# Sorted output experts of a two-layer attention kernel: the last pair's step moves into the next batch, tables are made later, one store per chunk

## The chip, the core and the metric

The kernel runs as one launch on one core of a Trainium2 chip. The metric is the device time of a launch in microseconds, lower is better. The core has five engines that run their own instruction streams and meet through semaphores: TensorE (PE: matmuls, and transposes done as matmuls), VectorE (DVE), ScalarE (ACT), GpSimd (POOL) and SyncE (SP, which here only issues transfers). PSUM is the accumulator memory, eight banks of 2 KB in each of 128 partitions; SBUF is the core's own memory, DRAM holds inputs, outputs and the scratch tables.

## The reference

Four batches of 512 tokens with 256 features go through two layers. The change touches the second step of the first layer:

```python
x = x + xattn(layernorm(x), ctx)               # one head, 1601 keys, softmax in fp32
# L0 ffn: 8 heads of 64, 8 experts per head
q, k = heads(x @ w_q), heads(x @ w_k)
gates = sigmoid(heads(x @ w_gate))             # (b, h, n, e)
gm = one_hot(argmax(gates, -1), 8) * gates     # one expert per head and token
values = einsum('bhne,ehdk,bnd->bhnk', gm, value_experts, x)
out = einsum('bhij,bhjk->bhik', softmax(causal(q @ k.T / 8)), values)
out = einsum('bhne,ehkd,bhnk->bhnd', gm, output_experts, out)
x = x + out.sum(axis=1)                        # sum over the heads
# then layer 1: 16-head attention over ctx with a mask, and a mixture of 32 experts
```

Every token picks one output expert in each head. Its row of 64 numbers is multiplied with that expert's 64x256 matrix alone, and the eight results are added to x.

## The kernel before

Everything here is in `attentions_ab`. For each batch b, TensorE runs `attention_a(b)` (the first attention, L766 scores, L779 transposes of probabilities, L798 context matmuls, L820), then `head_b(b)` (transposes of the normalised x at L867, gates at L874, queries and keys), then `attention_b(b)`: the 8 heads in four pairs. The value experts are 32 "units" of four 128x512 matmuls (L1056): eight before pair 0, and eight in each of pairs 0 to 2. VectorE takes each unit with the gates (L1511, L1515). Pair p's attention (transposes L929, value matmuls L1025) ends with `turn_rows`. The fourth pair (`last_pair`) has no units; the scores of the next batch's first tile stand between its parts.

In batches 0 to 2 (`SORTED` = 3) the output experts are done by sorting. Q = 4b + p numbers the pairs, EARLIER = 12. The steps of a pair:

- VectorE weighs the rows and writes them (`weigh`, `write_rows`, L1627). GpSimd scatters them to `sorted_in` in DRAM with eight indirect transfers (L677), to the places that the table `to_sorted` gives, so that blocks of 128 rows have one expert.
- SyncE loads for each of the 11 blocks and 2 heads of the pair the matrix of its expert, 22 transfers with an address read from the table `of_block` (`load_experts`, L605), and behind them the sorted rows (`load_sorted`, L615). The loads wait until the whole table is there, and until the blocks of pair Q-2 are multiplied.
- TensorE transposes the rows (`turn_sorted`, three groups, L970), ScalarE copies them out (`read_sorted`, L1365). TensorE multiplies two blocks at a time (`out_sorted`, six chunks c = 0 to 5, L992, bank 6 and 7), ScalarE copies each chunk out (`read_blocks`, L1379) and issues two stores of it to `sorted_out` (L1384). The buffers alternate, so a copy waits for the stores of the chunk two before.
- GpSimd gathers the results in the tokens' order (eight indirect transfers, L692, table `from_sorted`) once every store of the pair has landed (`all_kept`), and VectorE adds them to x (`add_back`, L1637).

TensorE's part of pair Q-1 stands in pair Q: pairs 0, 1 and 2 of a batch are multiplied in pairs 1, 2 and 3. Pair 3's part stands in `sorted_between(b + 1)`, between the next batch's `attention_a` and `head_b`, alone in its place. In `last_pair` ScalarE has all six chunks of pair 2 ahead of the next batch's first softmax (L1325; the maximum it needs is L1484). Batch 3 doesn't sort; it follows another scheme (`pair`, `ending_pair`).

The tables are made once a batch, by `place` on VectorE in five pieces, one behind each of the units 3 to 7 before pair 0 (L1573 to L1609; the last one, L1600 to L1609, gives `of_block`). They come from counts that TensorE makes by matmuls in bank 3. `placed` counts their 23 instructions. In batch 2 GpSimd normalises batch 0's x for the second layer (L146) behind `all_kept(7)`, TensorE transposes it at L820; the statistics for it (`statistics`) are taken on VectorE at the end of batch 1's pair 1. SyncE writes the finished x away in `keep_x`.

The context matmuls at L798 share bank 6 with the chunks: they wait for the same copies. `head_b` waits with its gates (bank 6) for the copies of all blocks so far.

## Time and profile before

| | us |
|---|---|
| median of 3 runs | 2146.98 |
| lowest, highest | 2142.21, 2147.06 |
| the profiled execution | 2155.61 |
| its span | 2153.8 |

The mean granted clock of TensorE is 0.95 of full speed. The rows below are of the profiled execution, in microseconds from the start of its span. The heads of batches 0 to 2 begin at 184, 419 and 683 (in the last two with the expert block of pair 3 ahead); behind 970 follow batch 3's experts and the second layer, which the diff doesn't touch.

### The profile page before, as it was taken

What the parts mean: (1) busy time and instruction counts of PE and PEld (TensorE: products, weight loads), DVE (VectorE), ACT (ScalarE), POOL (GpSimd) and SP (SyncE); (2) the same over time, 40 slices, a digit from 0 to 9 for tenths busy, and PEclk for the clock granted to TensorE, in tenths of its full rate; (3) what the DMA queues carried; (4) which work ended last, traced back from release to release, by engine and by line L of the source; (5) the groups of instructions that cost most, each with busy time, mean ns of one, the idle gap of its engine ahead of it and who ended that gap; (6) DMA issues with size and microseconds to landing.
All of it is one profiled execution on the core that took longest, in us unless ns stands there. A gap on an engine that the chain in (4) does not pass through costs nothing. (4 is left out here: it accounts for less than half of the span.)

```text
span 2153.8 us, 29336 instructions
## 1 busy us (share of the span) xinstructions
PE 1934.9 (90%) x10024; PEld 1024.5 (48%) x10024; DVE 1250.2 (58%) x2553; ACT 980.3 (46%) x1899; POOL 729.6 (34%) x660
## 2 busy tenths in 40 slices
PE   8989897988888888889998999999999999986993
PEld 5666344744456444565563333343343333335772
DVE  5434752266522665239877767778777877742342
ACT  3412242212323123222105879778877887861220
POOL 4330143104433054211106133224632541326575
PEclk9999998989989999899998999999999999997997
DMA  8741156214633046351125374337542643105997
GB/s 284 208 161 56 56 180 196 87 42 118 195 116 120 27 129 189 97 168 51 55 31 134 80 243 114 64 68 176 113 107 39 174 79 49 50 26 181 267 193 164
DMA packets 184077, 262.88 MB, mean 122 GB/s; under 512 B 48135, under 2 KB 140117, under 8 KB 182648
## 3 DMA queue, kind: packets, MB, share of 16 engines
q1 hardware_dynamic: 121208, 179.21, 30.9%
q0 software_dynamic: 26624, 47.18, 8.8%
q10 hardware_dynamic: 36096, 34.61, 4.9%
q8 instruction: 80, 1.31, 0.3%
q14 instruction: 69, 0.57, 0.1%
HBM read 165.92 MB, written 104.44 MB: 126 GB/s over the span
## 5 line engine op out<-in xcount | busy, mean ns | idle before, releaser
L2623 ACT ACTIVATE d_prob<-ps 128x512 f32<-128x512 f32 (+1 forms) x832 | 473.5, 597 | 155.2 <-PE ps L2473 154.4
L2650 DVE CUSTOM_DVE_ANT_0 ps<-ps,maskN 128x801 f32<-128x801 f32 x480 | 467.6, 1015 | 125.6 <-PE ps L2443 125.4
L1056 PE MATMUL ps<-vx_or_keys,b_xT 128*128 128x512 f32 x512 | 253.5, 623 | 19.1 <-DVE val_or_prob L1511 18.9
L2485 PE MATMUL ps<-d_prob,vaug 128*32 128x512 f32 (+1 forms) x1664 | 225.9, 609 | 0.3 <-ACT d_prob L2623 0.3
L692 POOL DMA_INDIRECT val_or_prob<-sorted_out,oxB x96 | 98.7, 1028 | 359.6 <-DVE xx L1637 160.7
L2472 PE MATMUL ps<-maskT,identb 128*128 128x512 bf16 (+1 forms) x498 | 192.0, 385 | 4.4 <-POOL maskT L2347 2.5
L2619 ACT CAST ps<-maskT 128x512 f32<-128x512 bf16 (+1 forms) x310 | 185.5, 598 | 0.0
L265 POOL DMA_INDIRECT table<-xr,slot x128 | 128.4, 1004 | 168.4 <-PE ps L2473 133.2
L1350 ACT ACTIVATE prob_or_gate<-ps,b_mx 128x512 f32<-128x512 f32 (+3 forms) x128 | 66.1, 525 | 187.8 <-DVE b_mx L1502 185.8
L1511 DVE TENSOR_TENSOR val_or_prob<-ps,b_gm 128x512 f32<-128x512 f32 x128 | 88.2, 689 | 103.4 <-PE ps L1056 101.6
L1056 PEld LDWEIGHTS ps<-vx_or_keys,b_xT 128*128 128x128 f32 x512 | 92.1, 195 | 114.1 <-issue 79.1
L1515 DVE TENSOR_REDUCE val_or_prob<-val_or_prob 128x64 f32<-128x512 f32 x128 | 132.4, 1034 | 4.4
L677 POOL DMA_INDIRECT sorted_in<-oxB x96 | 95.7, 997 | 110.0 <-DVE oxB L1627 81.4
L992 PE MATMUL ps<-oxB,og_or_pT 64*128 64x256 f32 x528 | 86.8, 452 | 41.8 <-ACT og_or_pT L1379 27.8
L2347 POOL TENSOR_SCALAR maskT<-c_rawT 128x512 bf16<-128x512 int32 (+1 forms) x52 | 100.2, 1926 | 50.9 <-PE ps L2473 43.2
L2473 PE MATMUL ps<-raw,kS 99*128 99x512 bf16 (+1 forms) x312 | 115.6, 387 | 1.4 <-ACT ps L2619 1.4
L2472 PEld LDWEIGHTS ps<-maskT,identb 128*128 128x128 bf16 (+1 forms) x498 | 49.7, 100 | 121.4 <-issue 34.2
L766 PE MATMUL ps<-maskN,kS 128*128 128x512 f32 (+1 forms) x256 | 101.3, 545 | 1.7 <-PEq L103 1.7
L2473 PE MATMUL ps<-qS,vx_or_keys 99*128 99x512 bf16 (+1 forms) x260 | 99.3, 386 | 1.9 <-ACT ps L2619 1.9
L2473 PE MATMUL ps<-vx_or_keys 99*128 99x512 bf16 (+1 forms) x260 | 98.3, 382 | 1.9 <-ACT ps L2619 1.9
L798 PE MATMUL ps<-og_or_pT,raw 128*128 128x128 f32 (+1 forms) x832 | 97.6, 275 | 0.0
L798 PEld LDWEIGHTS ps<-og_or_pT,raw 128*128 128x128 f32 (+1 forms) x832 | 95.4, 192 | 1.5 <-issue 1.5
(356 smaller groups left out, 3153.7 us busy)
## 6 DMA issues: line engine op xcount, KB each, us to landing
sorted_out<-og_or_pT ACTq DMA_DIRECT2D x90, 256.0 KB
oxB<-in_B_ox SPq DMA_DIRECT2D x264, 64.0 KB
c_rawT<-in_maskT SPq DMA_DIRECT2D x24, 512.0 KB
vx_or_keys<-k_parts SPq DMA_DIRECT2D x60, 200.1 KB, 7.1
k_parts<-x_k SPq DMA_DIRECT2D x16, 600.4 KB
table<-xr POOLq DMA_DIRECT2D x16, 578.0 KB
e_buf<-table SPq DMA_DIRECT2D x32, 289.0 KB, 4.0
oxB<-sorted_in SPq DMA_DIRECT2D x12, 704.0 KB, 5.4
```

The costliest lines, as they stand in the source:

```text
L265: g.indirect_dma_start(out=k.table[:, :], out_offset=bass.IndirectOffsetOnAxis(ap=k.slot[:, j:j + 1], axis=0), in_=k.xr[:, t, :], in_offse ...
L766: mm = pe.matmul(ps[:, i, 0:KC[i]], k.qkA[:, c, t * P:(t + 1) * P], k.ctxTA[:, c, i * BANK:i * BANK + KC[i]], start=c == 0, stop=c == NC - 1)
L798: mm = pe.matmul(ps[:, 6, m * P:(m + 1) * P], k.ctxNA[0:KW[i], i, m * P:(m + 1) * P], pT[0:KW[i], i, :], start=i == 0 and m == 0, stop=i = ...
L1056: mm = pe.matmul(ps[:, bank, :], xTB[:, c, t * P:(t + 1) * P], vxB[:, c, h, :], start=c == 0, stop=c == NC - 1)
L1515: v.tensor_reduce(val[:, t, h // 2 % 2, h % 2, :], tmp[:, u % 2, :].rearrange("p (e d) -> p d e", e=EB), AX_X, ALU.add).then_inc(val_sum, 1)
L2347: g.tensor_scalar(maskT[0:KW[i], i, :], rawT[0:KW[i], u % 2, i % 2, :], 0.0, MASKED, ALU.is_equal, ALU.mult).then_inc(biasT, 1)
L2472: pe.matmul(ps[0:w, BANKS[u], :], k.identb[0:w, 0:w], maskT[0:w, i, :], start=True, stop=False)
L2473: pe.matmul(ps[0:w, BANKS[u], :], kS[G % NS][0:KROWS + 3, h, i * P:i * P + w], qS[G % NS][0:KROWS + 3, h, :], start=False, stop=True, skip ...
L2485: mm = pe.matmul(ps[VW * h:VW * (h + 1), ACC, :], vaug[0:w, G % 2, i, h, :], prob[0:w, T % 2, h, :], start=i == 0, stop=i == NKT - 1)
L2619: nc.scalar.copy(ps[0:w, BANKS[later], :], maskT[0:w, i, :]).then_inc(mask_a, 1)
L2623: nc.scalar.activation(prob[0:w, T % 2, h, :], ps[0:w, BANKS[GH * T + h], :], ACT.Exp, scale=SCALE_C).then_inc(exped, 1)
L2650: v.tensor_tensor_reduce(banks, banks, maskN[:, t, MO[half]:MO[half] + w], 1.0, -3.0e38, ALU.add, ALU.max, mp[:, t, h, half:half + 1]).the ...
```

## The change

- Pair 3's sorted work is done in pair 0 of the next batch, in the places where pairs 1 and 2 have that of the pair before. `sorted_between` is left for batch 3 alone.
- Chunks 4 and 5 of pair 2 move from `last_pair` into the next `attention_a`; ScalarE copies them behind the softmax of tiles 0 and 1. The rest of `last_pair` is put in another order.
- Each chunk is stored with one transfer: the two heads' rows lie side by side in `sorted_out`. The table `from_sorted` goes, `to_sorted` serves both ways.
- GpSimd gathers tiles 0 and 1 before a pair's scatter, 2 and 3 behind it (in a batch's last pair all before). VectorE adds the later two in the next pair.
- Table pieces: the second moves from behind unit 4 to behind unit 5, the last three move into pair 0 (behind unit 9, unit 10 and the written rows). The counts are in bank 5.
- The statistics and `keep_x` move from pair 1 to pair 2. Head, GpSimd and VectorE waits are set to what is done by then.

```diff
-PLACING = 23
+PLACING = 21
...
-        to_sorted, from_sorted, of_block = ([x.bitcast(I32) for x in part[i:i + 2]] for i in (3, 5, 7))
+        to_sorted, of_block = ([x.bitcast(I32) for x in part[i:i + 2]] for i in (3, 5))
...
@@ sync
-                        if p == 1 and b >= 1:
+                        if p == 2 and b >= 1:
                             keep_x(b - 1)
@@ gpsimd, in gather: for t in tiles, in_offset from to_sorted
-                    if b >= 1 and p < 2:
-                        gather(PAIRS * b - 2 + p)
-                    if b < SORTED:
-                        if p >= 2:
-                            gather(PAIRS * b - 2 + p)
+                    Q = PAIRS * b + p
+                    if b == SORTED:
+                        if p < 2:
+                            gather(Q - 2, range(NT))
+                    else:
+                        ahead = 2 if p + 1 < PAIRS else NT
+                        if Q >= 2:
+                            gather(Q - 2, range(ahead))
                         scatter(b, p)
+                        if Q >= 2:
+                            gather(Q - 2, range(ahead, NT))
@@ tensor, attention_a
+                    if b and i == 1:
+                        out_sorted(PAIRS * b - 2, 4)
                     if i < NT and (b == 0 or i >= 1):
                         for j in range(NKC):
                             scores(b, i, j)
+                    if b and i == 1:
+                        out_sorted(PAIRS * b - 2, 5)
...
@@ tensor, head_b
-                pe.wait_ge(blocks_a, CHUNKS * PAIRS * b)
+                if b:
+                    pe.wait_ge(blocks_a, CHUNKS * (PAIRS * b - 1 if b < SORTED else PAIRS * b))
@@ tensor, turn_b; values gets the wait on placed
-                if g == 0 and p == 0 and b < SORTED:
-                    pe.wait_ge(placed, PLACING * b + 13)
...
@@ tensor, counts: bank 3 becomes bank 5
...
@@ tensor, sorted_pair (all nine places)
-                if p:
+                if Q:
                     turn_sorted(Q - 1, 0)
...
@@ tensor, last_pair
                 turn_sorted(Q - 1, 1)
+                turn_sorted(Q - 1, 2)
                 scores(b + 1, 0, 1)
                 turn_rows(b, p)
-                turn_sorted(Q - 1, 2)
+                out_sorted(Q - 1, 0)
                 scores(b + 1, 0, 2)
-                out_sorted(Q - 1, 0)
                 out_sorted(Q - 1, 1)
                 scores(b + 1, 0, 3)
-                for c in range(2, CHUNKS):
-                    out_sorted(Q - 1, c)
+                out_sorted(Q - 1, 2)
+                out_sorted(Q - 1, 3)
...
@@ tensor and scalar, the loop over batches
-                if b:
+                if b == SORTED:
                     sorted_between(b)
@@ scalar, attention_a, behind the softmax of tile i
+                    if b and i < 2:
+                        read_blocks(PAIRS * b - 2, 4 + i)
@@ scalar, read_blocks
-                    act.wait_ge(kept[c % 2], 32 * (n // 2))
+                    act.wait_ge(kept[c % 2], 16 * (n // 2))
+                if c == 0 and not between:
+                    act.wait_ge(placed, PLACING * ((Q + 1) // PAIRS + 1))
...
-                for a in range(2):
-                    half = k.sorted_out[Q % 2][ROWS * a:ROWS * (a + 1), :].rearrange("(j p) n -> p j n", p=P)
-                    nc.scalar.dma_start(half[:, 2 * c:2 * c + w, :], o[:, a, 0:w, :]).then_inc(kept[c % 2], 16)
+                nc.scalar.dma_start(k.sorted_out[Q % 2].rearrange("(j p a) n -> p j (a n)", p=P, a=2)[:, 2 * c:2 * c + w, :],
+                                    o[:, 0:w].rearrange("p j a n -> p j (a n)")).then_inc(kept[c % 2], 16)
@@ vector, sorted_pair
+                if p and Q >= 3:
+                    add_back(Q - 3, 2)
+                    add_back(Q - 3, 3)
+                if p == 0:
+                    place(b, 2)
                 weigh(b, p)
                 maxima(b, p + 1, 0)
                 unit(b, u + 2)
-                add(0)
+                if p == 0:
+                    place(b, 3)
+                if Q >= 2:
+                    add_back(Q - 2, 0)
                 unit(b, u + 3)
                 write_rows(b, p)
-                add(1)
+                if Q >= 2:
+                    add_back(Q - 2, 1)
+                if p == 0:
+                    place(b, 4)
...
-                add(3)
-                if Q == PAIRS + 1:
+                if Q == PAIRS + 2:
                     v.wait_ge(added, 2 * NT * PAIRS)
                     statistics(v, nq, k.xx[0][:, :, :])
```

TensorE, from the end of batch 0's last pair into batch 1's `attention_a`. L766 are scores, L992 the chunks (a row with x4 is one chunk of two blocks, x2 the last one), L779 the transposes of probabilities, L798 the context matmuls. Before:

```order
L766 MATMUL ps<-maskN,kS 128x512 x2
L992 MATMUL ps<-oxB,og_or_pT 128x256 x8
L766 MATMUL ps<-maskN,kS 128x65 x2
L992 MATMUL ps<-oxB,og_or_pT 128x256 x14
L779 MATMUL ps<-ident,val_or_prob 128x128 x8
L766 MATMUL ps<-maskN,kS 128x512 x6
L766 MATMUL ps<-maskN,kS 128x65 x2
L779 MATMUL ps<-ident,val_or_prob 128x128 x4
L798 MATMUL ps<-og_or_pT,raw 128x128 x16
L779 MATMUL ps<-ident,val_or_prob 65x128
L798 MATMUL ps<-og_or_pT,raw 128x128 x10
```

With the change (L774, L1003, L787 and L806 are the same lines moved; L965 is `turn_rows`):

```order
L1003 MATMUL ps<-oxB,og_or_pT 128x256 x4
L774 MATMUL ps<-maskN,kS 128x512 x2
L1003 MATMUL ps<-oxB,og_or_pT 128x256 x4
L774 MATMUL ps<-maskN,kS 128x65 x2
L1003 MATMUL ps<-oxB,og_or_pT 128x256 x8
L787 MATMUL ps<-ident,val_or_prob 128x128 x8
L1003 MATMUL ps<-oxB,og_or_pT 128x256 x4
L774 MATMUL ps<-maskN,kS 128x512 x6
L774 MATMUL ps<-maskN,kS 128x65 x2
L1003 MATMUL ps<-oxB,og_or_pT 128x256 x2
L787 MATMUL ps<-ident,val_or_prob 128x128 x4
L806 MATMUL ps<-og_or_pT,raw 128x128 x16
```

All six chunks stood ahead of the first probability transposes; now four do, one chunk stands behind the first transposes, and the last one (x2) behind the scores of tile 1, directly ahead of further transposes and the context matmuls.

TensorE, from the end of batch 1's `attention_a` into `head_b(1)`. L416 is the last of the attention, L867 (L879) the head's transposes. Before:

```order
L416 MATMUL ps<-bkA,b_kT 128x1 x8
L970 MATMUL ps<-ident,oxB 128x128 x11
L992 MATMUL ps<-oxB,og_or_pT 128x256 x22
L867 MATMUL ps<-ident,og_or_pT 128x128 x8
L874 MATMUL ps<-wgB,b_xT 128x64 x8
L884 MATMUL ps<-b_xT,wqB 128x512 x2
L884 MATMUL ps<-b_xT,wkB 128x512 x2
```

With the change:

```order
L820 MATMUL ps<-kS,og_or_pT 128x256 x2
L411 MATMUL ps<-b_kT,kS 128x512 x4
L416 MATMUL ps<-bkA,b_kT 128x1 x8
L879 MATMUL ps<-ident,og_or_pT 128x128 x8
L887 MATMUL ps<-wgB,b_xT 128x64 x8
L897 MATMUL ps<-b_xT,wqB 128x512 x2
L897 MATMUL ps<-b_xT,wkB 128x512 x2
```

The 11 transposes and 22 block matmuls between L416 and the head are gone from here.

VectorE, the last table piece of batch 1 (L1600, L1603, L1607, L1609). L1511 and L1515 take a unit. Before, ahead of pair 0:

```order
L1597 TENSOR_SCALAR oxB<-og_or_pT 128x16 x4
L1511 TENSOR_TENSOR val_or_prob<-ps,b_gm 128x512
L1515 TENSOR_REDUCE val_or_prob<-val_or_prob 128x64
L1600 TENSOR_TENSOR og_or_pT<-og_or_pT 128x64
L1603 TENSOR_TENSOR og_or_pT<-og_or_pT,oxB 128x704
L1607 TENSOR_REDUCE og_or_pT<-og_or_pT 128x88
L1609 TENSOR_SCALAR oxB<-og_or_pT 128x88
L1511 TENSOR_TENSOR val_or_prob<-ps,b_gm 128x512
L1515 TENSOR_REDUCE val_or_prob<-val_or_prob 128x64
```

With the change (the piece is L1613 to L1622; L1609 is the piece with `to_sorted`, L1650 `add_back`, L1640 the written rows, L1525 and L1529 a unit):

```order
L1609 TENSOR_SCALAR oxB<-og_or_pT 128x16 x2
L1650 TENSOR_TENSOR xx<-xx,val_or_prob 128x256 x2
L1525 TENSOR_TENSOR val_or_prob<-ps,b_gm 128x512
L1529 TENSOR_REDUCE val_or_prob<-val_or_prob 128x64
L1640 TENSOR_TENSOR oxB<-ps,b_gr 128x512
L1650 TENSOR_TENSOR xx<-xx,val_or_prob 128x256 x2
L1613 TENSOR_TENSOR og_or_pT<-og_or_pT 128x64
L1616 TENSOR_TENSOR og_or_pT<-og_or_pT,oxB 128x704
L1620 TENSOR_REDUCE og_or_pT<-og_or_pT 128x88
L1622 TENSOR_SCALAR oxB<-og_or_pT 128x88
L1525 TENSOR_TENSOR val_or_prob<-ps,b_gm 128x512
```

The table that the expert loads wait for is now complete behind the written rows of pair 0, and no longer behind unit 7.

## Rows read from the trace of the kernel before

**Rows 1.** Page, part 1: busy us (share of the span) xinstructions, by engine.

```profile
PE 1934.9 (90%) x10024; PEld 1024.5 (48%) x10024; DVE 1250.2 (58%) x2553; ACT 980.3 (46%) x1899; POOL 729.6 (34%) x660
```

**Rows 2.** Waits, PE, 180-970: engine line <- waited for: us, times, longest.

```profile
PE ps L992 <- ACT og_or_pT L1379: 27.8, 26, 1.9
...
PE ps L992 <- ACT val_or_prob L1379: 11.0, 10, 3.3
```

**Rows 3.** Timeline, PE (start, us, line, operation, count [idle before <- releaser]).

```profile
184.83 1.07 PE L867 MATMUL ps<-ident,og_or_pT 128*128 128x128 f32 x8
...
202.32 1.88 PE L1056 MATMUL ps<-vx_or_keys,b_xT 128*128 128x512 f32 x4
...
419.12 1.07 PE L970 MATMUL ps<-ident,oxB 128*128 128x128 f32 x8
...
454.38 1.88 PE L1056 MATMUL ps<-vx_or_keys,b_xT 128*128 128x512 f32 x4
...
682.81 1.07 PE L970 MATMUL ps<-ident,oxB 128*128 128x128 f32 x8
...
720.21 1.88 PE L1056 MATMUL ps<-vx_or_keys,b_xT 128*128 128x512 f32 x4
```

**Rows 4.** Timeline, ACT: the first softmax of batches 1, 2 and 3.

```profile
355.92 1.60 ACT L1325 ACTIVATE val_or_prob<-ps,a_mx 128x1601 f32<-128x1601 f32 x1 [1.78 <-issue]
...
615.26 1.60 ACT L1325 ACTIVATE val_or_prob<-ps,a_mx 128x1601 f32<-128x1601 f32 x1 [1.02 <-issue]
...
877.62 1.60 ACT L1325 ACTIVATE val_or_prob<-ps,a_mx 128x1601 f32<-128x1601 f32 x1 [0.97 <-ACT og_or_pT L1379]
```

**Rows 5.** Timeline, batch 2: ACT's second softmax, PE's first context matmuls.

```profile
628.67 1.60 ACT L1325 ACTIVATE val_or_prob<-ps,a_mx 128x1601 f32<-128x1601 f32 x1 [9.08 <-DVE a_mx L1484]
...
626.61 3.74 PE L798 MATMUL ps<-og_or_pT,raw 128*128 128x128 f32 x32
```

**Rows 6.** Timeline, batch 2: POOL normalises xx, PE transposes it.

```profile
619.42 4.85 POOL L146 TENSOR_SCALAR og_or_pT<-xx,norm_nc_mv,norm_nc_rstd 128x256 f32<-128x256 f32 x4 [6.06 <-DMA sorted_out<-og_or_pT]
...
630.19 0.60 PE L820 MATMUL ps<-ident,og_or_pT 128*128 128x128 f32 x4
```

**Rows 7.** Timeline, ACT, batch 3's block: two stores, a copy.

```profile
939.15 0.89 ACTq L1384 DMA_DIRECT2D sorted_out<-val_or_prob  x2
...
942.40 1.01 ACT L1379 COPY val_or_prob<-ps 128x1024 f32<-128x1024 f32 x1 [1.01 <-DMA sorted_out<-val_or_prob]
```

**Rows 8.** Timeline, SP's issues: slices and rows of pairs 0, 2, batch 0.

```profile
229.05 27.57 SPq L605 DMA_DIRECT2D oxB<-in_B_ox  x22
256.84 0.41 SPq L615 DMA_DIRECT2D oxB<-sorted_in  x1
...
324.45 30.20 SPq L605 DMA_DIRECT2D oxB<-in_B_ox  x22
```

**Rows 9.** Timeline, PE: pair 0's first sorted transposes, batches 0 and 2.

```profile
261.87 0.66 PE L970 MATMUL ps<-ident,oxB 128*128 128x128 f32 x4 [0.53 <-DMA oxB<-sorted_in]
...
781.66 0.66 PE L970 MATMUL ps<-ident,oxB 128*128 128x128 f32 x4 [3.70 <-DMA oxB<-sorted_in]
```

**Rows 10.** Timeline, DVE, batch 0: last table piece, rows of pairs 0, 1.

```profile
225.31 0.21 DVE L1600 TENSOR_TENSOR og_or_pT<-og_or_pT 128x64 f32<-128x64 f32 x1
...
227.40 0.20 DVE L1609 TENSOR_SCALAR oxB<-og_or_pT 128x88 int32<-128x88 f32 x1
...
243.47 0.68 DVE L1627 TENSOR_TENSOR oxB<-ps,b_gr 128x512 f32<-128x512 f32 x1
...
271.91 0.68 DVE L1627 TENSOR_TENSOR oxB<-ps,b_gr 128x512 f32<-128x512 f32 x1
```

**Rows 11.** Windows: us, busy of PE, PEld, DVE, ACT, POOL; PEclk; DMA; GB/s.

```profile
781.70:787.00 5.30, 5.30 (x16) 2.05 (x17) 1.23 (x1) 2.04 (x5) 0.00 (x0) 0.68 0.29 80
261.90:265.50 3.60, 3.60 (x14) 1.45 (x14) 2.55 (x5) 0.92 (x2) 0.00 (x0) 1.00 0.17 51
```

**Rows 12.** Timeline, PE, batch 1: first transposes of pair 2.

```profile
549.69 0.66 PE L929 MATMUL ps<-ident,prob_or_gate 128*128 128x128 f32 x4 [2.02 <-DVE b_pT L1714]
```

125 lines of the change are left out of this document (61 added, 64 removed).

## The prediction

> **What bounds the kernel now.** I read the page's engine line first, then TensorE's waits in the stage that holds the experts, then the timelines of the five engines there. TensorE is busy 90% of the span, no other engine above 58% [rows 1], so a change pays where it takes work or a wait off TensorE's row. In the stretch from the first gates to the last batch's head (180 to 970 us) TensorE waits 27.8 + 11.0 us in 36 places for ScalarE's copies of expert blocks [rows 2], and it waits for a batch's first softmax and for sorted rows to land [rows 4, 9]. These are what the change touches. Everything after 970 us should shift as a whole: nothing there is edited.
>
> All sums below are against the profiled execution (2155.61 us, span 2153.8), which lies 8.6 above the median of the runs, 2146.98; the difference found is then put on the median.
>
> **1. The block between attention and head goes, for batches 1 and 2.** In batch 0, which has no such block, the head takes 17.49 us from its first transpose (184.83) to the first value unit (202.32). In batches 1 and 2 the same way, with the last pair's expert block ahead of it, takes 454.38 - 419.12 = 35.26 and 720.21 - 682.81 = 37.40 us [rows 3]. Both should fall to 17.49, the waits for ScalarE's last blocks and for the input copied behind them included. Gain 17.77 + 19.91 = **37.7 us**. Batch 3 keeps its block.
>
> **2. The end of the last pair.** Today the batch's first softmax waits in ScalarE's queue behind six blocks and twelve stores: it starts at 355.92, 615.26 and 877.62, in the first two cases with no idle wait for its input [rows 4]. After, only four blocks stand ahead, with one store each. By my count ScalarE would be through with block 3 and its store at 346.1 (the 1.01 us copies, a 0.44 us issue each, matmuls of 1.13 us), and VectorE gives the maximum at about 345.8, since the gathers start some 1.6 us earlier once the last store is one issue and no load of sorted rows competes with it. The softmax starts near 346.1, 606.3 and 868.9. Gain 9.8 + 9.0 + 8.7 = **27.5 us**.
>
> **3. Chunks 4 and 5 come back in the attention.** Chunk 4 costs TensorE 1.07 us. Chunk 5 stands behind the scores of tile 1, and it brings a new wait: the context matmuls (L798) write bank 6 and wait until every block of that pair is copied out. ScalarE copies chunk 5 only after the softmax of tile 1. In batch 2 that softmax ends at 630.27, and the context matmuls start at 626.61 [rows 5]; a one-block copy (0.59 us, half of 1.01 and some start cost) and the signals would free them at 631.0. So 1.1 + 4.4 = 5.5 us a batch, three times: **16.5 us** lost. Queued behind the waiting matmul is TensorE's whole attention.
>
> **4. Batch 2's normalisation of the kept input.** GpSimd normalises xx for the next layer only when all stores of that pair have landed. Today this ends at 624.27, before its transpose (L820, 630.19) [rows 6]. After, the store of chunk 5 goes out at about 632.5, lands 2.3 us later (as the quiet stores of batch 3 do: issue ends 940.04, the next copy it gates starts 942.40 [rows 7]), and 4.85 us of normalising follow [rows 6]: some 639.8. TensorE comes there at 635.7. **4.1 us** lost.
>
> **5. Tables made later: the large cost.** SyncE loads the 22 expert slices of a pair in one loop, each with an address read from the table, and only behind them in its queue the sorted rows. The loop starts about 1 us after the last table instruction and takes 27.6 to 30.2 us [rows 8]. In batch 0 the table is done at 227.60 (227.40 + 0.20), the slices are issued from 229.05 to 256.62, the rows at 256.84, and TensorE takes them at 261.87 after a 0.53 us wait [rows 8, 9]. So 34.3 us from table to rows, and this chain already ends last: in batch 2 TensorE waits 3.70 us there [rows 9]. The scatter, which batches 1 and 2 also wait for, comes clear of it after the change. Now the table's last piece (225.31 to 227.60, 2.29 us [rows 10]) moves from before pair 0 to behind that pair's rows.
> Where does it end? From the first value unit of the batch, the units reach pair 0's last transpose group in 28.2 us (31.4 today in batch 0, with three pieces of table between the units on VectorE; I take 1.5 us off for the last unit, 1.1 for VectorE being free for the transposes' copies, and leave half of the low clock). In batch 0 VectorE then goes through pair 0 as now (write of the rows ends at 244.15, 10.4 us behind that group [rows 10]) and needs 2.3 us more: 28.2 + 12.6 = 40.8. Plus 34.3: 75.1 us against 59.55 today (261.87 - 202.32), so 15.5 later. In batches 1 and 2 pair 0 has the sorted work too, like pair 1 of batch 0, where the write of rows starts at 271.91: 28.2 + 14.65 + 34.3 = 77.15 against 61.45 in batch 2 (781.66 - 720.21 [rows 3, 9]), and I take batch 1 alike: 15.7 later each. Total **46.9 us** lost. That is net of the sooner units, and it hides all TensorE work that the change adds to pair 0 (11 transposes and 22 blocks): the wait in pair 1 grows to some 12 us in batches 1 and 2 and 18 in batch 0. The later pairs have slack again: SyncE's loop for pair 1 starts right behind, and is through 5 us before its rows are wanted.
>
> **6. The clock.** After its 3.70 us of waiting the stretch from the sorted transposes to the value matmuls takes 5.3 us where batch 0, after 0.53, needs 3.6, at a granted clock of 0.68 against 1.00 [rows 9, 11]: a level between 1.2 and 2.4 GHz on average. Batch 0 now pays such a stretch, and waits of 12 to 18 us may cost up to 3 us, nearly twice that. I take 2.5 for batch 0, 0.9 more for each of batches 1 and 2, and 3.9 for the four new waits of points 3 and 4: **8.2 us** lost. On this the Trainium skill (TensorE: Matmul & The Clock Gate, Why this matters for your kernels) says that idle gaps between bursts of matmuls return TensorE to the half rate; the trace agrees on 5.3 against 3.6 us.
>
> **7. One store per chunk, gathers, statistics.** An issue takes 0.44 us on ScalarE (0.89 for two [rows 7]), and one of two goes. Most waits for block copies are for work ahead of the copy, not for the store, so I take 1.5 us in the pairs and 2.0 in batch 3's block. Moving the statistics of xx from pair 1's end to pair 2's removes a 2.02 us wait and the slow unit behind it [rows 12]: 2.4. Gathers split around the scatters cost nothing: GpSimd's waits are in front of its scatters, and the additions fit into VectorE's gaps. Gain **5.9 us**. The Trainium skill (DMA: Bandwidth & Descriptors, Anatomy of one DMA) puts most of a transfer's fixed 2.0 us into the write's receipt, none of which a merged store saves; by it only the issue is gained, as taken here.
>
> **Sum:** -37.7 - 27.5 + 16.5 + 4.1 + 46.9 + 8.2 - 5.9 = +4.6 us. Profiled 2160.2; on the median **2151.6 us**, 0.2% slower, which a measurement cannot tell from no change (0.3%, 6.4 us).
>
> **Rivals.**
> A, slower: the clock. If each of the seven long waits costs 3.3 us, twice the 1.7 of rows 11, and SyncE's loop runs at its 30.2 us beside stores and scatters rather than 27.6, that is 7 x 3.3 - 8.2 = 15 and 3 x 2.6 = 8 more: up to 2174; half of it gives 2163. It decides from 1.8 us beyond my sum, where 2153.4 is passed. For it: the second loop, beside scatters, does take 30.2 us [rows 8]. Against: the loop of pair 0 is the quickest one now.
> B, faster: stores bind. If half an issue and a quicker landing count at each of 36 block waits (38.8 us [rows 2]), 0.45 x 36 = 16 us go instead of 3.5: 2139. For it: a copy of a block waits 1.01 us for a store's landing [rows 7]. Against: in the pairs most of them wait for TensorE.
> C, the gains come whole and the table's delay is hidden (rows could be loaded without waiting for the slices): 2146.98 - 50 = 2097. Against it is SyncE's order, unchanged: slices, then rows. I give it 3%.
>
> **Chances.** My sum 60%, A 20%, B 17%, C 3%. The case of my sum spans 2145 to 2158 and passes 2153.4 a quarter of the time, so it gives 0.45 to no change and 0.15 to slower; B gives 0.01 to no change. Same 0.46, slower 0.15 + 0.20 = 0.35, faster 0.16 + 0.03 = 0.19. The range that holds 8 in 10 reaches into A and B: 2138 to 2166.
>
> **What would show it.** The profile after should have TensorE's first sorted transposes in pair 1 wait 15 to 19 us in batch 0 and 10 to 14 in batches 1 and 2, for the load of sorted rows; no expert block between the attention and the head of batches 1 and 2, and 17.5 us for that head; about 3.3 us of waiting ahead of L798's first context matmul of batches 1 to 3; some 4 us ahead of the transpose of the kept input. I am wrong if the wait in pair 1 stays under 8 us (then faster), or if new waits appear in pairs 2 and 3 (then slower).

## The result

The changed kernel is slower than the one before: 2171.86 us (median; 2168.06 to 2175.55) against 2147.02 (2142.21 to 2151.10), a ratio of 1.0116 with a 95% interval of 1.0086 to 1.0147. The forecast was 2151.6 with a range of 2138 to 2166: it expected a difference too small to measure, and the time lies above the range. The profiled execution took 2168.06 us, its span is 2166.2. That is 12.4 more than the span before; up to the first value unit of batch 3, where the edited part ends, it is 20.8 us behind (987.18 against 966.36). The part behind it was 8.4 us shorter in this execution than in that of before, which lay 8.6 above its own median; that part took 1177 to 1185 us in the traces of the first eight experiments, so it varies by that much from one execution to the next. So the 20.8 us are what has to be explained, and they are close to the 24.8 between the medians.

TensorE's waits in the edited stretch of the changed kernel (engine, line, waited for: us, times, longest); the lines answer to [rows 2]:

```profile
PE ps L981 <- DMA oxB<-sorted_in: 51.3, 5, 17.3
PE ps L1003 <- ACT og_or_pT L1394: 23.4, 24, 1.6
PE ps L787 <- ACT val_or_prob L1338: 13.0, 3, 5.9
...
PE ps L806 <- ACT og_or_pT L1394: 10.3, 3, 3.4
...
PE ps L1003 <- ACT val_or_prob L1394: 2.3, 4, 1.2
```

L1003 is L992 of before, L787 L779, L806 L798, L981 L970. The waits for block copies fell from 38.8 to 25.7 us. The wait for sorted rows was before, from 180 to 970 us:

```profile
PE ps L970 <- DMA oxB<-sorted_in: 8.9, 5, 3.7
```

It rose from 8.9 to 51.3 us, and 10.3 us are new ahead of the context matmuls.

TensorE's timeline: heads and first units of batches 1 and 2 (answering to [rows 3]), and pair 0's sorted rows in each batch with the value matmuls behind the first ([rows 9]).

```profile
277.31 1.12 PE L981 MATMUL ps<-ident,oxB 128*128 128x128 f32 x4 [17.32 <-DMA oxB<-sorted_in]
...
283.11 2.38 PE L1038 MATMUL ps<-b_pT,val_or_prob 128*64 128x512 f32 x16
...
438.06 1.07 PE L879 MATMUL ps<-ident,og_or_pT 128*128 128x128 f32 x8
...
455.56 1.88 PE L1069 MATMUL ps<-vx_or_keys,b_xT 128*128 128x512 f32 x4
...
535.13 1.11 PE L981 MATMUL ps<-ident,oxB 128*128 128x128 f32 x4 [14.13 <-DMA oxB<-sorted_in]
...
704.68 1.07 PE L879 MATMUL ps<-ident,og_or_pT 128*128 128x128 f32 x8
...
722.18 1.88 PE L1069 MATMUL ps<-vx_or_keys,b_xT 128*128 128x512 f32 x4
...
801.78 1.11 PE L981 MATMUL ps<-ident,oxB 128*128 128x128 f32 x4 [13.87 <-DMA oxB<-sorted_in]
```

Both heads take 17.50 us, where 35.26 and 37.40 were. The three waits for rows are 17.32, 14.13 and 13.87 us; forecast were 15 to 19 and twice 10 to 14.

The end of the table on VectorE, and SyncE's loop and load behind it ([rows 8, 10]):

```profile
243.41 0.20 DVE L1622 TENSOR_SCALAR oxB<-og_or_pT 128x88 int32<-128x88 f32 x1
...
498.62 0.20 DVE L1622 TENSOR_SCALAR oxB<-og_or_pT 128x88 int32<-128x88 f32 x1
```

```profile
245.06 27.13 SPq L608 DMA_DIRECT2D oxB<-in_B_ox  x22
272.25 0.57 SPq L618 DMA_DIRECT2D oxB<-sorted_in  x1
...
499.73 29.83 SPq L608 DMA_DIRECT2D oxB<-in_B_ox  x22
529.66 0.53 SPq L618 DMA_DIRECT2D oxB<-sorted_in  x1
```

From batch 0's first unit (202.74) to the end of the table are 40.87 us (forecast: 40.8). In batch 1 (455.56 to 498.82) they are 43.3, forecast 42.85. The loop took 27.13 us in batch 0, but 29.83 in batch 1, and 29.83 in batch 2.

The first softmax of batch 2, with what stands ahead of it on ScalarE and on VectorE ([rows 4]):

```profile
622.23 1.01 ACT L1394 COPY og_or_pT<-ps 128x1024 f32<-128x1024 f32 x1 [1.97 <-DMA sorted_out<-og_or_pT]
...
625.63 1.60 ACT L1338 ACTIVATE val_or_prob<-ps,a_mx 128x1601 f32<-128x1601 f32 x1 [2.39 <-DVE a_mx L1498]
```

```profile
622.53 0.88 DVE L1650 TENSOR_TENSOR kS<-kS,val_or_prob 128x256 f32<-128x256 f32 x2 [1.47 <-DMA val_or_prob<-sorted_out,oxB]
```

The second softmax of batch 1, ScalarE's copy of chunk 5 behind it, and TensorE's context matmuls ([rows 5]):

```profile
382.30 1.60 ACT L1338 ACTIVATE val_or_prob<-ps,a_mx 128x1601 f32<-128x1601 f32 x1 [6.00 <-DVE a_mx L1498]
...
383.89 0.58 ACT L1394 COPY og_or_pT<-ps 128x512 f32<-128x512 f32 x1
```

```profile
384.61 5.31 PE L806 MATMUL ps<-og_or_pT,raw 128*128 128x128 f32 x32 [3.42 <-ACT og_or_pT L1394]
```

Set side by side, the stages of the two profiled executions, each from the start of one TensorE or ScalarE instruction to the next, give the account. "Forecast" is the prediction's own terms, with its 8.2 us of clock put where it put them.

```
us, changed minus before                          forecast   measured
head and block, batches 1 and 2                     -37.7      -37.7   (17.76 + 19.90)
value matmuls of pair 3 -> first softmax            -27.5      -21.9   (8.56 + 5.98 + 7.36)
first softmax -> end of the attention, 3 times      +24.5      +23.6   (6.16 + 11.50 + 5.98)
first unit -> first sorted rows, 3 times            +46.9      +51.4   (15.0 + 18.2 + 18.2)
sorted rows -> value matmuls of pair 1               +4.3       +4.6   (2.16 + 1.31 + 1.11)
value matmuls of pair 1 -> those of pair 3           -3.9       +2.0   (+3.74 - 4.37 + 2.64)
batch 3's block and head, and the start              -2.0       -1.3
sum                                                  +4.6      +20.7
```

The single differences stand in brackets, in the batches' order. No row is off by more than 6 us, but three are off by 4.5 to 6 to the same side. Whether the mechanisms behind the rows are the right ones, a comparison of two executions doesn't tell; the experiments do.

### The profile page after: what moved, and what is told of

Read it like the earlier page. It is cut to its first block and busy times, and to the rows that moved or that the text cites. A ratio compares the mean times of both kernels' runs of the same rounds, so it can differ in the third digit from the quotient of the medians.

```text
span 2166.2 us, 29178 instructions
## 1 busy us (share of the span) xinstructions
PE 1915.9 (88%) x9944; PEld 1020.7 (47%) x10024; DVE 1249.3 (58%) x2547; ACT 979.2 (45%) x1899; POOL 729.4 (34%) x660
## 5 line engine op out<-in xcount | busy, mean ns | idle before, releaser
L1069 PE MATMUL ps<-vx_or_keys,b_xT 128*128 128x512 f32 x512 | 252.3, 621 | 13.0 <-DVE val_or_prob L1525 12.4
L2488 PE MATMUL ps<-maskT,identb 128*128 128x512 bf16 (+1 forms) x425 | 163.4, 385 | 1.8 <-DVE d_oN L2698 1.7
L1525 DVE TENSOR_TENSOR val_or_prob<-ps,b_gm 128x512 f32<-128x512 f32 x128 | 88.2, 689 | 121.3 <-PE ps L1069 121.1
L1529 DVE TENSOR_REDUCE val_or_prob<-val_or_prob 128x64 f32<-128x512 f32 x128 | 132.5, 1035 | 4.4
L806 PE MATMUL ps<-og_or_pT,raw 128*128 128x128 f32 (+1 forms) x832 | 103.8, 285 | 10.3 <-ACT og_or_pT L1394 10.3
L806 PEld LDWEIGHTS ps<-og_or_pT,raw 128*128 128x128 f32 (+1 forms) x832 | 101.5, 202 | 12.4 <-issue 12.4
L1394 ACT COPY og_or_pT<-ps 128x1024 f32<-128x1024 f32 x66 | 62.2, 942 | 96.5 <-PE ps L1003 74.8
L1003 PE MATMUL ps<-oxB,og_or_pT 64*128 64x256 f32 x528 | 79.1, 416 | 26.3 <-ACT og_or_pT L1394 23.4
```

The costliest lines, as they stand in the source:

```text
L806: mm = pe.matmul(ps[:, 6, m * P:(m + 1) * P], k.ctxNA[0:KW[i], i, m * P:(m + 1) * P], pT[0:KW[i], i, :], start=i == 0 and m == 0, stop=i = ...
L1069: mm = pe.matmul(ps[:, bank, :], xTB[:, c, t * P:(t + 1) * P], vxB[:, c, h, :], start=c == 0, stop=c == NC - 1)
L1529: v.tensor_reduce(val[:, t, h // 2 % 2, h % 2, :], tmp[:, u % 2, :].rearrange("p (e d) -> p d e", e=EB), AX_X, ALU.add).then_inc(val_sum, 1)
L2488: pe.matmul(ps[0:w, BANKS[u], :], k.identb[0:w, 0:w], maskT[0:w, i, :], start=True, stop=False)
```

## Experiments

All times are medians. The kernel before ran beside each: 2145.0 us on the chip of the first four, 2146.3 on that of the next four. Differences between versions on these two chips, and to the changed kernel's 2171.9 us on a third, are good to 5 or 6 us by the spread of the runs. Diffs are against the changed kernel and cut to what matters ("..." and "@@" mark the cuts); the counts that waits compare with were changed to match.

**The tables made early again.** The pieces of `place` go back to where they stood, all else as changed.

```diff
                 unit(b, 4)
+                place(b, 1)
                 maxima(b, 0, 2)
                 unit(b, 5)
-                place(b, 1)
+                place(b, 2)
                 unit(b, 6)
+                place(b, 3)
                 unit(b, 7)
+                place(b, 4)
...
-                if p == 0:
-                    place(b, 2)
...
```

> The changed kernel, but with the five table pieces on VectorE where they stood before (behind units 3 to 7); all else as changed. Theory (the late table is the loss): TensorE's waits of 17.3, 14.1 and 13.9 us at pair 0's sorted rows nearly go (2 us left of the first), and with them some 4 us of low clock behind them: 2171.9 - 15 - 14 - 14 - 4 = 2125 us, below the kernel before. Rival (the same waits come back in the later pairs, since SyncE's loop for pair 1 can't start before the blocks of the last pair are multiplied): 2140 to 2150. Rival (the table is not what the rows wait for): 2172.

Measured: 2123.95 us, ratio 0.9889 (0.9853 to 0.9925). That is 48 us below the changed kernel and faster than the kernel before. TensorE's waits for sorted rows:

```profile
PE ps L981 <- DMA oxB<-sorted_in: 8.4, 4, 2.8
```

51.3 us have become 8.4, and the stretch behind the waits takes 3.61, 3.61 and 3.64 us in the three batches. The late table is the loss, and its size was forecast well: 46.9 + 4.3 against 48. The rival, that the waits come back in later pairs, falls: from the value matmuls of pair 1 to those of pair 3 the three batches take 207.2 us instead of 204.2.

**Rows ahead of the slices.** The prediction's rival C supposed rows that needn't wait for the expert slices. This makes it so, with late tables.

```diff
-                        load_experts(b, p)
                         load_sorted(b, p)
+                        load_experts(b, p)
```

> The changed kernel, but SyncE issues the load of a pair's sorted rows ahead of its 22 expert slices. The tables stay late. Theory (the rows are late because they stand behind the slices in SyncE's queue): the waits of 17.3, 14.1 and 13.9 us shrink to about 2 us each, some of it comes back as a wait for slices at chunk 0 in each pair, 3 to 8 us in the later ones: about 2145 us. Rival (the slices become the bound everywhere, the wait only moves to chunk 0): 2165 or more. If the queue's order had no part in it: 2172.

Measured: 2213.66 us, ratio 1.0306 (1.0269 to 1.0343). My expectation was wrong by nearly 70 us, and the rival was right. The waits for rows are gone, and chunk 0 waits instead, in two pairs of each batch and for 9.9 to 16.9 us:

```profile
PE ps L1003 <- issue: 84.7, 7, 16.9
```

"Issue" stands there because the transposes that the matmul also waits for were long done: by the kernel's code chunk 0 alone waits for the slices, so it is these that are missing. They can't start before the scatter has ended, and SyncE's 27 to 30 us then come on top of the scatter instead of running beside it. SyncE's queue is the resource, not the place of the rows in it.

**Gathers unsplit.** All gathers ahead of the scatter, the additions behind the third, fourth, sixth and eighth unit of a pair as before.

```diff
-                        ahead = 2 if p + 1 < PAIRS else NT
                         if Q >= 2:
-                            gather(Q - 2, range(ahead))
+                            gather(Q - 2, range(NT))
                         scatter(b, p)
-                        if Q >= 2:
-                            gather(Q - 2, range(ahead, NT))
```

> The changed kernel, but all gathers of a pair stand ahead of its scatter and the additions stand where they were before. Theory (the gathers behind the scatter compete with the load of sorted rows, whose landing took 8.5 to 10.4 us in the last pairs against 5.5 before): the waits of 2.5 and 3.5 us at the last pairs' sorted rows go, and two slow stretches of 2 us behind them: 2164 us. Rival (SyncE's loop for that pair ends too late anyway): 2170 to 2174, waits unchanged.

Measured: 2169.70 us (2168.47 to 2175.38), ratio 1.0104 (1.0068 to 1.0140). The load of sorted rows, changed kernel, and then this one (issue to landing):

```profile
DMA to landing us min/median/max: 4.4/7.0/10.4
```

```profile
DMA to landing us min/median/max: 4.6/5.4/11.7
```

The median landing went from 7.0 to 5.4 us, and the waits at the last pairs' rows in batches 0 and 2 nearly went with it. Changed kernel, then this one:

```profile
347.55 1.11 PE L981 MATMUL ps<-ident,oxB 128*128 128x128 f32 x4 [2.50 <-DMA oxB<-sorted_in]
...
873.26 1.11 PE L981 MATMUL ps<-ident,oxB 128*128 128x128 f32 x4 [3.46 <-DMA oxB<-sorted_in]
```

```profile
349.56 0.66 PE L978 MATMUL ps<-ident,oxB 128*128 128x128 f32 x4 [0.59 <-DMA oxB<-sorted_in]
...
872.29 0.66 PE L978 MATMUL ps<-ident,oxB 128*128 128x128 f32 x4 [0.58 <-DMA oxB<-sorted_in]
```

So the theory has the mechanism and the rival, which said that the waits stay, only the time: 2.2 us, within the intervals. The pairs did gain. From the value matmuls of pair 1 to those of pair 3 the three batches take 197.9 us, where the changed kernel takes 204.2 and the kernel before 202.2. In this one execution the 6.3 us came back elsewhere: 3.4 us ahead of the first unit, where the two kernels are alike, 3.1 us in the head of batch 1 (20.59 us) and 4.2 ahead of batch 3's first softmax.

**TensorE kept busy while it waits.** Matmuls of the transposed input with the identity go into bank 5, which is free there; nobody reads them.

```diff
                 if g == 0:
+                    if Q % PAIRS == 0:
+                        pe.wait_ge(bo_ev, Q + 1)
+                        pe.wait_ge(placed, PLACING * (Q // PAIRS + 1))
+                        for _ in range(34 if Q == 0 else 28):
+                            pe.matmul(ps[:, 5, :], k.ident[:, :], xTB[:, 0, :], start=True, stop=True)
                     pe.wait_ge(ld_sorted, 16 * (Q + 1))
```

> The changed kernel with 34 (batch 0) or 28 (batches 1 and 2) added 128x512 matmuls into a free bank while TensorE waits for pair 0's sorted rows; they add work to the computation, which nobody reads. They take some 16 and 13 us, within the waits. Theory (a long wait costs low clock behind it): the stretch from the sorted transposes to the value matmuls falls from 5.8, 6.6 and 6.4 us to 3.6, 5.3 at most, in all 4 to 5 us: 2167 us. Rival (the clock is no part of the loss): 2172; if the added matmuls outlast the waits: above 2172.

Measured: 2193.01 us. I had mis-sized the filler: 34 of these matmuls (68 in the trace, two for each) took 29.35 us, not 16.

```profile
261.80 29.35 PE L976 MATMUL ps<-b_xT,ident 128*128 128x512 f32 x68
```

The overshoot is 12.0 + 10.1 + 10.3 = 32.4 us and the time rose by only 21, so something was given back. The same with 19 and 15:

> The changed kernel with 19 (batch 0) or 15 (batches 1 and 2) added 128x512 matmuls in TensorE's waits for pair 0's sorted rows, whose results nobody reads; 0.863 us each as the run with 34 and 28 of them shows, so 16.4 and 12.9 us, inside the waits of 17.3, 14.1 and 13.9. Theory (a long wait costs low clock behind it): 4 to 5 us less than the changed kernel from the stretches behind the waits, up to 10 if later waits shrink too (in the run with too many, 32 us of excess work cost only 21): 2162 to 2168. Rival (no price of the clock): 2172.

Measured: 2171.02 us (2166.31 to 2172.38), no different from the changed kernel. Yet in the trace the stretch from the sorted rows to the value matmuls fell from 5.80, 6.59 and 6.39 us to 3.64, 3.64 and 3.63, 7.9 us in all. The windows of batch 0's stretch (us, busy of PE, PEld, DVE, ACT, POOL, PEclk, DMA share, GB/s) and of batch 1's head, changed kernel first:

```profile
277.00:284.00 7.00, 6.69 (x18) 2.73 (x20) 1.98 (x3) 2.03 (x5) 0.00 (x0) 0.65 0.22 57
437.00:460.00 23.00, 22.17 (x81) 11.60 (x81) 10.57 (x17) 3.67 (x8) 4.27 (x4) 1.00 0.08 23
```

```profile
277.00:284.00 7.00, 6.24 (x33) 2.83 (x34) 2.97 (x3) 2.21 (x6) 0.00 (x0) 1.00 0.21 59
437.00:460.00 23.00, 22.17 (x63) 11.77 (x63) 8.46 (x15) 3.52 (x7) 4.27 (x4) 0.85 0.08 24
```

The granted clock behind the wait goes from 0.65 to 1.00, and that of batch 1's head from 1.00 to 0.85: the head takes 20.8 us there instead of 17.5, and the same in batch 2, and batch 3's block and head take 35.9 instead of 32.5. So the low level (1.2 of 2.4 GHz) does show behind a long wait, but taking that stretch away made another one slow, and the total did not move. The clock that the forecast charged to these waits can't be called their price.

**Chunk 5 copied ahead of the softmax.** On top of early tables.

```diff
                         turned_probabilities(T, 1)
+                    if b and i == 1:
+                        read_blocks(PAIRS * b - 2, 5)
...
-                    if b and i < 2:
-                        read_blocks(PAIRS * b - 2, 4 + i)
+                    if b and i == 0:
+                        read_blocks(PAIRS * b - 2, 4)
```

> The kernel with early tables, and ScalarE copies chunk 5 ahead of the softmax of tile 1, not behind it. Theory (the context matmuls wait for that copy): TensorE's 10.3 us there go, the wait for the normalised input (3.9 us) goes with them, and up to 1.6 us of low clock in each of three places: 2124 - 10 - 4 - 3 = 2107 us. Rival (the softmax of tile 1 comes later for it and the wait only changes its name): 2120 to 2124.

Measured: 2118.33 us (2117.41 to 2122.14), ratio 0.9868 (0.9829 to 0.9907): 5.6 below the early tables, where 17 were expected. In batch 2:

```profile
601.91 3.81 PE L806 MATMUL ps<-og_or_pT,raw 128*128 128x128 f32 x32 [0.19 <-ACT og_or_pT L1396]
609.25 1.11 PE L828 MATMUL ps<-ident,og_or_pT 128*128 128x128 f32 x4 [3.53 <-POOL og_or_pT L146]
```

The 3.4 us ahead of L806 are down to 0.2, in all three batches, so that mechanism is as forecast. The wait for the kept input is not gone (3.53 us): GpSimd still waits for chunk 5's store. And the two heads have become slow. Batch 1's, in the kernel with early tables and in this one (us, busy of PE, PEld, DVE, ACT, POOL, PEclk, DMA share, GB/s):

```profile
420.54:438.03 17.49, 16.66 (x58) 8.80 (x58) 7.55 (x13) 3.52 (x7) 4.26 (x4) 1.00 0.11 30
```

```profile
415.04:435.86 20.82, 19.99 (x58) 11.05 (x58) 7.56 (x13) 3.52 (x7) 4.33 (x4) 0.84 0.08 25
```

From the softmax to the next head (in batch 3 to the block) the three batches take 4.8, 3.9 and 5.4 us less, 14.1 in all, and the heads take 3.3, 3.1 and 1.2 us more, at a lower granted clock: the same as with the filled waits. 6.4 us are left of 14.1, close to the 5.6 between the medians (each of the two versions ran on one chip, and their intervals leave 1 to 10). So here, too, the low clock went from one place to another.

**All six chunks in the last pair.** Also on top of early tables.

```diff
@@ tensor, attention_a
-                    if b and i == 1:
-                        out_sorted(PAIRS * b - 2, 4)
...
-                    if b and i == 1:
-                        out_sorted(PAIRS * b - 2, 5)
@@ tensor, last_pair
-                out_sorted(Q - 1, 2)
-                out_sorted(Q - 1, 3)
+                for c in range(2, CHUNKS):
+                    out_sorted(Q - 1, c)
@@ scalar: read_blocks(.., 4 + i) out of attention_a, and
-                    if behind and more:
+                    if behind:
                         for c in range(4, CHUNKS):
```

> The kernel with early tables, but with all six chunks of pair 2 in the last pair again, as in the kernel before (one store each, the new order of the rest kept). Theory (by the traces, the move of the two chunks into the attention gave 22 us at the softmax and took 24 in the attention): within 5 us of 2124, 2119 to 2126. By the forecast's own terms (27.5 gained, 20.6 lost and 4 of clock) it would be 2127. Rival (copies and stores of two more chunks, 3.2 us each, stand ahead of each batch's softmax and nothing comes back): 2124 + 3 x 6.4 = 2143.

Measured: 2106.77 us (2103.88 to 2113.08), ratio 0.9813 (0.9770 to 0.9856), 17 us below the version with the two chunks in the attention. Neither the theory nor the rival nor the forecast's terms had that. The stages, from the starts in the traces, in us:

```
                                     before                early tables          + six chunks
value matmuls, pair 3 -> softmax     25.3  24.1  23.8      16.4  16.8  18.2      21.5  19.9  21.6
softmax -> next head                 (with the block)      69.4  79.3  71.9      62.2  66.6  64.0
```

In the second row batch 3's value counts its block up to the head's transposes. Two readings. First, 10.2 of the 21.9 us that the changed kernel gains ahead of the softmax are there without the move of the chunks; they belong to the rest of the change, the single stores and the order of the last pair above all. Second, the move itself gained only 11.6 us there and cost 27.9 behind: 7.2, 12.8 and 7.9. In batch 2 the transpose of the kept input, here with no wait at all:

```profile
603.77 0.60 PE L828 MATMUL ps<-ident,og_or_pT 128*128 128x128 f32 x4
```

The two traces also tell what the 27.9 us are. The waits ahead of L806 are 10.3 us and that for the kept input 3.9. The two chunks themselves hold TensorE for 7.7 us, since chunk 4 takes 1.8 to 2.0 us there (1.1 at the full clock). And the context matmuls behind the waits take 5.2 to 5.4 us instead of 3.74, in batch 2 twice: 6.4 us. That is 28.3.

**Two stores per chunk**, on top of early tables.

```diff
-                nc.scalar.dma_start(... [:, 2 * c:2 * c + w, :], o[:, 0:w] ...).then_inc(kept[c % 2], 16)
+                for a in range(2):
+                    nc.scalar.dma_start(... [:, 2 * c:2 * c + w, a, :], o[:, 0:w, a, :]).then_inc(kept[c % 2], 16)
```

> The kernel with early tables, but with two stores of 1 KB rows per chunk in place of one of 2 KB rows. Theory (only the issue is saved, and mostly under other waits): 3 to 5 us slower, 2128 us. Rival (stores bind at each of 36 block copies, 0.45 us each): 2140 us.

Measured: 2131.95 us (2127.91 to 2133.61), ratio 0.9929 (0.9900 to 0.9958). One store per chunk is worth about 8 us, between the theory (3 to 5) and the rival (16). The two versions ran on different chips, and the spread of their runs leaves 3 to 13, so the 3.5 us that the forecast gave it are low but not excluded.

**The block between attention and head kept.** Undone alone (late tables), and on top of early tables and six chunks.

```diff
@@ tensor, sorted_pair (nine places); scalar: behind = p >= 1
-                if Q:
+                if p:
@@ tensor and scalar, the loop over batches
-                if b == SORTED:
+                if b:
                     sorted_between(b)
```

> Early tables, six chunks in the last pair, and the last pair's sorted work between attention and head again in every batch; what is left of the change is one store per chunk, the split gathers, the moved statistics and the last pair's order. Theory (the move pays 37.7 us at the heads of batches 1 and 2, and costs 5.2 us in each of their pairs 0, which take 66.5 instead of 61.4 us up to the first sorted rows): 2106.8 + 37.7 - 10.3 = 2134 us. Rival (pair 0 hides the moved work wholly): 2144. Rival (the block was mostly covered by other waits): under 2120.

> The changed kernel (late tables) with one part undone: the last pair's sorted work stands between attention and head again in every batch. Theory (with late tables pair 0 hides the moved work wholly, so the move pays the full 37.7 us; without it the tables come 2 us sooner in two batches): 2171.9 + 37.7 - 4 = 2206 us. Rival (the move pays the same with late tables as with early ones, 28 us by the forecast of the early pair): 2200. Rival (it pays little): below 2185.

Both ran on other chips, on which the kernel before takes 2265 to 2281 us, 5.5 to 6.3% more than on the first. So only ratios and comparisons on one chip are used. Measured for the first: 2254.43 us, ratio 0.9945 (0.9913 to 0.9977), where 2134 against 2146 is 0.9944; for the second 2316.74, ratio 1.0151 (1.0123 to 1.0180), where the theory's 2206 is 1.028 and the last rival, that the move pays little, reaches up to 1.018 and has it. The first one was run again beside the second:

> Early tables, six chunks in the last pair, the block between attention and head kept; once more, because the chip of its first run took 2265 us for the kernel before, and SyncE's loops took longer there. Theory, as for the first run: 2134 us where the kernel before takes 2146 (ratio 0.9945 was measured on that other chip). Rival (pair 0 hides the moved work wholly): 2144. Rival (the block was mostly covered by other waits): under 2120.

It gave 2268.27 us, ratio 0.9930 (0.9888 to 0.9972). The changed kernel and three others then ran side by side on one such chip:

> The changed kernel unaltered, beside the next three on one chip. If the chip takes some 2146 us for the kernel before: 2172 us (ratio 1.0116). If it is one on which SyncE's loops take 31 us and more and the kernel before over 2260: the late tables cost more, ratio 1.010 to 1.02.

> Early tables and six chunks in the last pair, all else as changed. 2107 us (ratio 0.981) where the kernel before takes 2146; 65 us below the changed kernel on the same chip.

> As the last one, with the block between attention and head kept. Theory (the move pays 37.7 us and costs 10.3 in the pairs 0): 27 us above the last one. Rival (pair 0 hides the moved work wholly): 38 above. Rival (mostly covered): within 13 us.

> The changed kernel, late tables, with only the block between attention and head kept. Theory (late tables hide the moved work, so the move pays nearly the full 37.7 us): 34 us above the changed kernel on the same chip. Rival (as much as with early tables): 27 above. On the chip of its first run it was 48 above the kernel with early tables, six chunks and the block.

```
                                        us        ratio to before (2266.93 us)
changed                                 2283.59   1.0098 (1.0064 to 1.0132)
changed, block kept                     2302.12   1.0184 (1.0136 to 1.0232)
early tables, six chunks                2238.71   0.9897 (0.9855 to 0.9938)
early tables, six chunks, block kept    2250.93   0.9919 (0.9881 to 0.9958)
```

SyncE's loops for pairs 0 and 1 of batch 1 in the changed kernel on that chip, where the first chip took 29.83 and 27.91 us:

```profile
524.15 36.01 SPq L608 DMA_DIRECT2D oxB<-in_B_ox  x22
...
561.63 36.07 SPq L608 DMA_DIRECT2D oxB<-in_B_ox  x22
```

Here each of the 22 addresses and issues takes up to 1.6 us, instead of 1.2 to 1.4. TensorE takes 41 to 46 us from one pair's value matmuls to the next instead of 31 to 35. The loops are not all that sets these chips apart. In the version with early tables and six chunks TensorE hardly waits for sorted rows there (3.5 us). It waits for block copies, and the copies and VectorE's products of the units wait for a signal of which the profile doesn't name the source ("remote"):

```profile
PE ps L999 <- ACT og_or_pT L1388: 56.6, 29, 8.0
PE ps L999 <- issue: 25.5, 7, 8.1
PE ps L977 <- DMA oxB<-sorted_in: 3.5, 1, 3.5
```

```profile
ACT og_or_pT L1388 <- remote: 92.1, 17, 9.9
```

```profile
DVE val_or_prob L1519 <- remote: 82.9, 10, 12.2
```

Such waits for copies stand in all ten traces from these chips (60 to 92 us in each) and in none from the chips of the first eight experiments. They are not waits for slices: the long "issue" waits at L999 (3.0 to 8.1 us) stand at chunk 2, directly behind such a copy, and by the code chunk 0 alone waits for slices. What holds the signal up stays open.

The move of the block pays 18.5 us with late tables and 12.2 with early ones; the spread of the runs leaves some 15 and 13 us to either side, so the second is not clear of nothing. Expected were 34 and 27. The rival "within 13 us" has the second number, and with early tables and six chunks the gain over the changed kernel is 44.9 us, not 65. Why the move pays less there was not found; the loops and the waits above are both at hand. The two versions with the block ran once more, beside 2269.96 us for the kernel before:

> Early tables, six chunks in the last pair, the block kept. If the kernel before takes some 2146 us: 2134 by the price of the move worked out from the traces of the first chips (37.7 - 10.3 us over 2106.8), 2144 if pair 0 hides the moved work wholly, under 2120 if the block was mostly covered. If it takes over 2260: ratio 0.992 to 0.995, as twice before.

> Late tables with the block kept, all else as changed. If the kernel before takes some 2146 us: 2206 us (the moved work is hidden by the wait for the rows, and the move pays 34); rival 2199 (it pays 27, as with early tables). If it takes over 2260: ratio 1.015 to 1.018, as twice before.

Measured: 2262.64 us, ratio 0.9969 (0.9935 to 1.0003), a little above the 0.992 to 0.995 expected, and 2312.03, ratio 1.0181 (1.0143 to 1.0220), as expected. No run shows what the move pays on the first chips. It can be estimated from the traces: 37.7 us at the two heads, less 5.2 us in each of the two pairs 0, where the version with early tables and six chunks takes 66.6 and 66.5 us from the first unit to the sorted rows of pair 1, against 61.3 and 61.5 before. That makes 27 us. It supposes that nothing else there hangs on the block, and the slower chip, with 12 us, doesn't bear it out.

**Gathers unsplit with early tables and six chunks**, beside the first run with the block.

> Early tables, six chunks in the last pair, and all gathers of a pair ahead of its scatter, the additions where they stood before. Theory (the split gathers neither gain nor cost more than 3 us, as with late tables, 2169.7 against 2171.9): 2104 to 2110 us. Rival (with early tables the last pairs' rows bind, and gathers behind the scatter slow their landing, 8 to 10 us against 5.5): 2098 to 2102. Rival (scatters that stand behind all gathers come later, and the rows with them): above 2112.

Measured: 2218.04 us, ratio 0.9795 (0.9770 to 0.9819). The split version had 0.9897 (0.9855 to 0.9938) on a like chip. So on these chips the split gathers may cost 1%; the two were not run side by side, and what does it was not tried.

## Why the forecast was wrong

The mechanisms were right, late tables above all. Three terms of the sum were mis-sized, all to the same side, and make 16 us of the 20.3 between 2151.6 and 2171.9: the softmax start of point 2 (5.6 us), "Plus 34.3" in point 5 (4.5), and the later pairs, where point 7 has "Gathers split around the scatters cost nothing" and point 5 "The later pairs have slack again" (5.9). The other 4 us are the difference between two executions and two medians. In the order of the points:

1. **The block at the heads:** right to 0.1 us, both heads 17.50.
2. **The end of the last pair:** 27.5 us forecast, 21.9 measured. The failed step is that the softmax starts when ScalarE has counted through four blocks, 15.4, 15.2 and 15.1 us behind the value matmuls of pair 3, with the maximum ready just before. ScalarE was through after 16.6, 16.2 and 16.3 us, 3.4 us later in all; its fourth copy first waits 1.3 to 2.0 us for a store to land. And the maximum comes last in all three batches, since VectorE stands in front of it waiting for gathered rows (4.7, 1.5 and 3.2 us): 2.2 us more, nearly all in batch 2, where the softmax waits 2.39. Nearly half of the gain is also not the move's (10.2 of 21.9, by the run with six chunks).
3. **Chunks 4 and 5 in the attention:** the wait at bank 6 was named with its size (3.4 us measured, 3.3 named, 4.4 counted in the sum), and with points 4 and 6 the stretch was right, 24.5 forecast and 23.6 measured. What the forecast didn't have is how little the move buys: the term of 16.5 us was held against a gain of 27.5, and by the run with six chunks the move brought 11.6 and cost 27.9.
4. **The kept input:** right in kind; 2.1 us with late tables, 3.9 with early ones, forecast 4.1.
5. **Late tables:** right in mechanism and place. The time from first unit to table was forecast to 0.5 us. The step that was off is "Plus 34.3", taken from batch 0 for all: there it was 33.7 (243.61 to 277.31), in batch 1 36.3 (498.82 to 535.13), because the loop took 29.83 us and not 27.6. That is rival A's second half, and 4.5 us of the error.
6. **The clock:** the stretches behind the waits were slow, as forecast (4.6 against 4.3 us), but the filled waits show that removing them gains nothing in the end. A term that had its size and not its meaning. Rival A rests on it with its larger half, so that its 2163 to 2174 holds the measured time is in large part luck.
7. **Stores, gathers, statistics:** forecast -5.9, of which 3.9 between the value matmuls of pairs 1 and 3; there the changed kernel lost 2.0. New waits of 2.5 and 3.5 us stand at the sorted rows of pair 2 in batches 0 and 2, the sign of being wrong that the forecast itself had named. With unsplit gathers they are 0.6 each and the stretch is 4.3 us shorter than in the kernel before, so the stores and the statistics brought there about what was forecast, and the split gathers took 6.3 us from it. In batch 0 the rows are issued at 338.22 and taken 9.3 us later, unsplit at 344.08 and 5.5 us later; the forecast counted a landing at 5.0. Since the whole time stayed the same without the split, this says where the forecast's row was wrong and not that unsplitting pays.

Rival C's "- 50" doesn't follow from the terms either: without the late tables and the clock behind them the sum is -46.6, some 2100 us. The run with early tables took 2124.

The account by changes, on the first chips: late tables +48 and the two chunks in the attention +17, each by a run; single stores -8, by a run, 3 to 13; the block's move -27, an estimate from traces that no run bears out; and the rest, by difference, -5. The sum is +25, measured +24.8. How the 32 us are shared between the last two is not shown. The forecast had the largest loss and the largest gain nearly right and called the difference nothing. Two chunks in another place, the smallest-looking part of the change, were booked as a gain of some 3 to 11 us and are a loss of 17.

The version with early tables and six chunks (0.9813) beats the kernel before by 1.9% and the changed one by 3.0%; on the slower chip by 1.0% and 2.0%.

## What to carry to other kernels

When an edit moves the point from which a queue with a fixed length of work can start, count from that point through the queue to the first reader: here 34 us from the table through the address reads, the issues and the rows' landing made one late table cost what the whole rest had won. Split a gain at a join by its causes before you charge one of them to a moved step: work taken off a queue ahead of a wait gains only until the other input of that wait is last, while work put behind it pays in full. A slow stretch seen behind a wait is not yet a price of the wait; fill the wait and look at the total.

## What I had not expected of the hardware

- The same program differs by 5.6% between chips (2146 against 2267 us for the kernel before), and in the trace of the changed kernel the loop of dynamic issues is longer by a fifth (29.83 against 36.01 us for 22 transfers, in batch 1), while TensorE's head of batch 2 takes 17.50 us on both.
- Filling three waits took 7.9 us of low clock from behind them and gave it back at two heads (17.5 to 20.8 us each) and elsewhere; the total stayed at 2171 us. Taking three other waits away (chunk 5 copied early) made the same two heads slow, 20.8 and 20.6 us.
- A 128x512 fp32 matmul of the filler took 0.863 us (29.35 for 34).
